# Routed expert block: second group of tiles ranked and scattered before the list begins, copies of the transposes a step later

## The reference, cut to what matters

```python
x = x + tanh(g_xattn) * softmax(mask(scale * (q @ k.T) * layernorm(x)))   # 4 x 512 x 512
h = layernorm(x)                                          # 2048 tokens of 512
w = sigmoid(h @ Wg.T); top 2 of 8 experts by w + bias     # weights divided by their sum
y = sum over a token's two experts: w_e * (silu(h @ W1_e.T) * (h @ W3_e.T)) @ W2_e.T
x = x + tanh(g_ffn) * y
```

## Time and profile before

| | |
|---|---|
| median of 3 timed runs | 350.49 us (348.11 to 350.96) |
| the profiled execution's own time | 346.8 us |
| its span | 344.9 us |
| TensorE matmuls busy | 286.4 us (83%) |
| VectorE, ScalarE, GpSimd busy | 191.1, 127.8, 195.0 us |
| software DMA queue (GpSimd's) | 9760 packets, 20.49 MB, 38.6% of 16 engines |

### The profile page before, as it was taken

The page is one execution under the profiler, slowest core; times in us unless marked ns, Lnnn a source line. Parts: engine busy times, 40 slices in busy tenths (PEclk is TensorE's granted clock), DMA queues, the critical chain, the costliest instruction groups (busy, mean ns, idle before and its releaser), DMA issues.

```text
span 344.9 us, 5188 instructions
## 1 busy us (share of the span) xinstructions
PE 286.4 (83%) x1316; PEld 204.4 (59%) x1316; DVE 191.1 (55%) x496; ACT 127.8 (37%) x239; POOL 195.0 (57%) x208
## 2 busy tenths in 40 slices
PE   4889898489876497678776799999999999999981
PEld 1244454245435375565564577888888888888860
DVE  2697868999946287565233325454454454454530
ACT  2678577237626233022122122333323333323320
POOL 5198997266884616616587355635656535664313
PEclk9999899658865599989989999999999999999998
DMA  7999889955833521945669376856666654865345
GB/s 225 331 416 323 269 291 361 291 184 134 158 105 93 141 74 8 62 57 93 63 66 97 30 121 119 130 115 121 114 104 107 115 105 80 153 112 104 56 62 61
DMA packets 27026, 48.69 MB, mean 141 GB/s; under 512 B 9524, under 2 KB 10296, under 8 KB 25976
## 3 DMA queue, kind: packets, MB, share of 16 engines
q0 software_dynamic: 9760, 20.49, 38.6%
q1 hardware_dynamic: 14408, 15.04, 13.6%
q10 hardware_dynamic: 2832, 12.85, 12.3%
HBM read 28.51 MB, written 19.85 MB: 140 GB/s over the span
## 4 chain that ended last, share of the span: by engine, by line
DMA 47%; issue 22%; POOL 12%; DVE 9%; PE 5%; POOLq 2%; ACT 1%; SPq 1%; ACTq 0%; DVEq 0%
DMA out<-rows,slot 29%; DMA out<-rows 8%; POOL rows L439 5%; DMA slot_table<-entry,slot_index 4%; POOL out L458 3%; DMA rows<-in_x 3%; POOL slot_table L426 3%; PE bank L895 2%; DVE rows L691 1%; DVE w_lo L830 1%; POOLq L450 1%; DMA rows<-xn_rows,slot 1%; DMA w_hi<-in_ctx_t 1%; DVE w_hi L668 1%; DVE bn L661 1%
## 5 line engine op out<-in xcount | busy, mean ns | idle before, releaser
L458 POOL DMA_INDIRECT out<-rows,slot x39 | 62.1, 1592 | 75.0 <-DMA out<-rows,slot 37.4
L809 DVE TENSOR_TENSOR xt_lo<-bank,xt_hi 128x512 fp32r<-128x512 f32 x39 | 27.0, 691 | 77.6 <-ACT xt_hi L581 66.3
L984 PE MATMUL bank<-w_hi,xt_hi 128*128 x156 | 65.2, 418 | 0.6 <-issue 0.6
L986 PE MATMUL bank<-w_hi,xt_lo 128*128 x156 | 61.4, 394 | 0.0
L985 PE MATMUL bank<-w_lo,xt_hi 128*128 x156 | 61.4, 393 | 0.0
L602 ACT ACTIVATE rows<-bank,slot 128x512 f32<-128x512 f32 x39 | 26.8, 688 | 73.9 <-DMA out<-rows,slot 40.1
L439 POOL DMA_INDIRECT rows<-xn_rows,slot x39 | 39.2, 1004 | 22.9 <-issue 15.2
L589 ACT ACTIVATE rows<-bank 128x256 f32<-128x256 f32 x39 | 15.0, 385 | 81.2 <-PE bank L986 60.7
L426 POOL DMA_INDIRECT slot_table<-entry,slot_index x32 | 32.9, 1028 | 17.5 <-issue 8.9
L1011 PE MATMUL bank<-w_hi,gt_hi 128*128 x78 | 31.7, 406 | 13.3 <-DVE gt_lo L826 13.3
L815 DVE SCALAR_TENSOR_TENSOR rows<-rows,bank 128x256 f32<-128x256 f32 x39 | 16.3, 418 | 34.5 <-ACT rows L589 32.1
(11 more groups left out here) (128 smaller groups left out, 464.6 us busy)
## 6 DMA issues: line engine op xcount, KB each, us to landing
w_lo<-in_w ACTq DMA_DIRECT2D x8, 1024.0 KB, 7.0
xn_rows<-w_hi SPq DMA_DIRECT2D x17, 256.0 KB, 8.9
rows<-in_x SPq DMA_DIRECT2D x16, 256.0 KB, 4.7
out<-rows SPq DMA_DIRECT2D x16, 256.0 KB, 4.0
w_lo<-in_w ACTq DMA_DIRECT2D x8, 512.0 KB, 5.8
w_hi<-in_ctx_t SPq DMA_DIRECT2D x4, 256.0 KB, 5.4
slot<-slot_table SPq DMA_DIRECT2D x39, 1.0 KB, 2.7
rows<-xn_rows,slot POOLq DMA_INDIRECT x39
```

Of the source, the lines that this page charges most:

```text
L458: pool.indirect_dma_start(out=out[0:SPARE + P * READY[segment(i)], :], out_offset=bass.IndirectOffsetOnAxis(ap=slot[:, i, 0:1].bitcast(U32 ...
L809: dve.tensor_tensor(xt_lo[:, i % 2].rearrange("p k s -> p (k s)"), ps_x[i % 2][:], xt_hi[:, i % 2].rearrange("p k s -> p (k s)").bitcast(F32),
L984: pe.matmul(ps_h[i % 2][:], xt_hi[:, i % 2, k, :], hi, start=(k == 0), stop=False)
L986: mm = pe.matmul(ps_h[i % 2][:], xt_lo[:, i % 2, k, :], hi, start=False, stop=(k == KC - 1))
```

## The change

- The scatters of group 0 are issued in steps 9 to 12 instead of 10 to 13 (`SCATTERS`). SyncE waits for them and loads the slots of the first seven entries one step sooner, ahead of its store of tile 14.
- Group 1 is ranked, weighted and given its slots by VectorE right behind the last residual, before the low parts of the first two gathered entries and the last splits. TensorE counts its positions behind the first gathered transpose, into a bank of their own. GpSimd issues six of its eight scatters behind gather 3 (new call), the other two with entry 0, ahead of addition 0.
- Group 2's ten scatters are spread over entries 4 to 10 (2, 1, 2, 1, 2, 1, 1) instead of 4 to 8 (two each).
- ScalarE copies the transposes of a tile one step later, right behind the exponentials; TensorE makes the logits of a tile behind the spins instead of at the step's start. One weight piece is split a step sooner, and the splits stand ahead of the router's tanh.

```diff
--- before.py
+++ after.py
@@ -52,13 +52,13 @@
     READY = (7, 11, TILES)
     UNITS = 3 * E
     PIECE = W13 // 2
-    SPLITS = (1, 1, 2, 2, 1, 2, 1, 2, 1, 1, 1, 2, 1, 1, 1, 2)
+    SPLITS = (1, 1, 2, 2, 1, 2, 1, 2, 1, 1, 1, 2, 1, 1, 2, 1)
     LO_BY_POOL = (0, 1, 2, 4, 6, 7, 9, 10)
     LOADS = {0: (2,), 1: (3,), 2: (4,), 4: (5,), 5: (6,), 6: (7,), 7: (8,), 8: (9, 10, 11), 9: (12,), 10: (13,), 11: (14,),
              12: (15,)}
-    SCATTERS = {10: (0, 0, 3), 11: (0, 3, 6), 12: (0, 6, 10), 13: (0, 10, 14)}
-    LATE_SCATTERS = {0: (1, 0, 4), 1: (1, 4, 6), 2: (1, 6, 8), 4: (2, 0, 2), 5: (2, 2, 4), 6: (2, 4, 6), 7: (2, 6, 8),
-                     8: (2, 8, 10)}
+    SCATTERS = {9: (0, 0, 3), 10: (0, 3, 6), 11: (0, 6, 10), 12: (0, 10, 14)}
+    LATE_SCATTERS = {0: (1, 6, 8), 4: (2, 0, 2), 5: (2, 2, 3), 6: (2, 3, 5), 7: (2, 5, 6), 8: (2, 6, 8), 9: (2, 8, 9),
+                     10: (2, 9, 10)}
     SPINS = 5
     SLOT_SEMS = 16
     ROWS = (E - 1) * REGION + LIST * P
@@ -175,7 +175,7 @@
         bank = [psum(f"bank{i}") for i in range(8)]
         ps_s = bank[0:2]
         ps_neg, ps_t, ps_early, ps_q, ps_k, ps_l = bank[2:]
-        ps_pos = (ps_early[:, 0:(MOST + 1) * E],) + 2 * (ps_l[:, 2 * P:2 * P + (MOST + 1) * E],)
+        ps_pos = (ps_early[:, 0:(MOST + 1) * E], ps_neg[:, 0:(MOST + 1) * E], ps_l[:, 2 * P:2 * P + (MOST + 1) * E])
         ps_h = bank[0:2]
         ps_g = bank[2]
         ps_x = (bank[4], bank[6])
@@ -362,7 +362,8 @@
                     store_xn(step - 2)
                 if 2 <= step and step - 2 + XR < TILES:
                     reuse_x(step - 2)
-                if step == TILES:
+                if step == TILES - 1:
+                    listed(0)
                     for i in range(4):
                         load_slots(i)
                 if 1 <= step <= TILES:
@@ -370,8 +371,6 @@
                 if step % NT == 3 and step // NT + 2 < B:
                     load_ctx(step // NT + 2)
                 if step == TILES - 1:
-                    listed(0)
-                elif step == TILES:
                     for i in range(4, FIRST[1]):
                         load_slots(i)
             for k in (1, 2):
@@ -503,6 +502,7 @@
             normed(TILES - 1)
             gather(2)
             gather(3)
+            enter_slots(1, 0, 6)
             for i in range(LIST):
                 if i + 4 < LIST:
                     gather(i + 4)
@@ -625,19 +625,23 @@
             act.activation(tg[:], gb_sb[:, 0:2], ACT.Tanh).then_inc(s_tg, 1)
             for step in range(TILES):
                 exponentials(step)
+                if step >= 2:
+                    transposed(step - 2)
+                for unit in units_in(step)[0:2]:
+                    if unit != 2 * E + 4:
+                        split_hi(unit)
                 if step == END[0] + 1:
                     router_tanh(0)
                 elif step == END[1] + 1:
                     router_tanh(1)
-                for unit in units_in(step):
-                    split_hi(unit)
                 squares(step)
-                if step >= 1:
-                    transposed(step - 1)
+                if step == TILES - 2:
+                    split_hi(2 * E + 4)
                 if step % NT == 2 and step // NT + 1 < B:
                     project(step // NT + 1)
                 for n in LOADS.get(step, ()):
                     load_weights(n)
+            transposed(TILES - 2)
             split_hi(UNITS - 2)
             gathered_hi(0)
             transposed(TILES - 1)
@@ -859,23 +863,19 @@
                 elif step == END[0] + 2:
                     router_slots(0)
                     list_tiles(0)
-            for unit in units_in(TILES - 1):
+            router_ranks(1)
+            router_weights(1)
+            gathered_lo(0)
+            router_slots(1)
+            gathered_lo(1)
+            for unit in range(2 * E + 5, UNITS):
                 split_lo(unit)
-            gathered_lo(0)
-            split_lo(UNITS - 2)
-            gathered_lo(1)
-            split_lo(UNITS - 1)
-            router_ranks(1)
             for i in range(LIST):
                 gate_rows(i)
                 if i + 2 < LIST:
                     gathered_lo(i + 2)
-                if i == 0:
-                    router_weights(1)
                 gated_transposed(i)
                 if i == 0:
-                    router_slots(1)
-                elif i == 1:
                     list_tiles(1)
                 elif i == 2:
                     router_ranks(2)
@@ -941,6 +941,8 @@
                 counts = where[:, n * E:(n + 1) * E]
                 pe.wait_ge(s_chosen, 3 * g + 3)
                 pe.wait_ge(s_slots, 2 * g)
+                if g == 1:
+                    pe.wait_ge(s_zmax, TILES)
                 pe.matmul(counts, ones[:], chosen_sum[:], start=True, stop=False)
                 for t in range(n):
                     pe.matmul(counts, ones[:], chosen[:, start + t, :], start=False, stop=(t == n - 1))
@@ -991,7 +993,7 @@
                 if i > 0:
                     pe.wait_ge(s_gt, 2 * i)
                 else:
-                    pe.wait_ge(s_zmax, TILES)
+                    pe.wait_ge(s_slots, 4)
                 for c in range(FC):
                     mm = pe.transpose(ps_g[:, c * P:(c + 1) * P], gate[:, i % 2, c * P:(c + 1) * P], ident[:])
                 mm.then_inc(s_g, 1)
@@ -1023,8 +1025,6 @@
             pe.wait_ge(s_wg_in, 16)
             projected = 1
             for step in range(TILES):
-                if step >= 2:
-                    logits(step - 2)
                 if step + 1 < TILES:
                     scores(step + 1)
                     masks(step + 1)
@@ -1032,6 +1032,8 @@
                     positions(0)
                 if step < TILES - 2:
                     spin(projected)
+                if step >= 2:
+                    logits(step - 2)
                 if step >= 1:
                     transpose(step - 1)
                 if step % NT == 2 and step // NT + 1 < B:
@@ -1039,6 +1041,7 @@
                     projected += 1
             logits(TILES - 2)
             gathered(0)
+            positions(1)
             transpose(TILES - 1)
             gathered(1)
             pe.wait_ge(s_lo_pool, len(LO_BY_POOL))
@@ -1052,7 +1055,6 @@
                     gathered(2)
                 elif i == 1:
                     gate_transpose(0)
-                    positions(1)
                     gathered(3)
                     output(0, last)
                     gate_transpose(1)
```

## The result

The changed kernel takes 337.88 us (median of 4 runs, 335.28 to 338.05) against 349.30 us for the kernel before (4 runs, 348.11 to 350.96): a ratio of 0.9637, 95% interval 0.9571 to 0.9702, or 11.4 us less. The direction held. The profiled execution of after took 335.28 us with a span of 333.3, 11.6 us less span than before.

What follows compares the result with a forecast made beforehand. Bound: the chain of scatter-additions until entry 11, TensorE behind it. The ruling V falls from 210.6 to 203.55, 7.0 us, taking the profiled 346.8 to 339.8 and the median to 343.5; own range 340 to 347, wide range 336.5 to 351.

Steps and rivals of the forecast that it cites:

- V(11): V for addition 11, landing at 213.35 us: 203.55, forecast to rule in place of addition 8's 210.6.
- V: Earliest place of entry 11 on TensorE's 4.76 us line if addition a lands at t: t + 4.5 - 4.76 (a - 8).
- gather 7's wait: GpSimd's 5.41 us stall for group 1's slots before gather 7, forecast to go.
- new wait at gather 15: GpSimd idles some 6 us for the slots of group 2's last scatter, gather 15 going at 201.45 us.
- cost of additions 3 to 8 behind scatters: List, GpSimd: 7.46 us per addition behind a pair, 6.65 behind one scatter, 42.3 in all; addition 8 lands at 194.1.
- Gather 0 goes at about 107: Start of the list: group 0's last scatter issued near 96, landing 5.6 us later; gather 0 at 107 instead of 113.33.
- The main loop: Later copies, logits and earlier scatters: net taken as 0, bounds 2 us earlier to 3.5 us later.
- ScalarE's wait at L544 near 98 gone: Sign that the forecast is right: ScalarE no longer waits 3.53 us for tile 12's transpose in the main loop.
- Quick: Rival, chance 0.20: a single scatter among additions costs the chain nothing and lands like a gather; 336.5 to 340 us.
- no stall at gather 15: Sign that the forecast is wrong and the quick rival holds: GpSimd does not wait before gather 15.
- Flat: Rival, chance 0.22: main loop costs 3.5 us and the list starts later; 3.5 us won, 347, down to nothing.
- slower: Rival, chance 0.13: scatter ahead of gather 15, single scatters hold every addition 8.86 us; 4.1 us slower, 354.6 us.

Runs made afterwards that it cites:

- u_second: Changed kernel with group 1 ranked and scattered where it was before, all else as changed: 346.65 us, ratio 0.993 to the kernel before.
- only_second: Kernel before with group 1's part of the change alone: 338.26 us against 348.14, ratio 0.973.
- only_spread: Kernel before with group 2's scatters spread as in the change, nothing else: 350.70 us against 347.58, ratio 1.008.
- no_scatter2: Changed kernel without group 2's ten scatters and SyncE's wait for them, leaving out some tokens' expert rows: 324.03 us, ratio 0.930 to the kernel before.
- u_spread: Changed kernel with group 2's scatters in pairs at entries 4 to 8 again: 336.89 us, ratio 0.963 to the kernel before.
- sooner: Changed kernel with group 2's scatter pattern one entry sooner, entries 3 to 9: 337.98 us, ratio 0.970 to the kernel before.
- after_again: The changed kernel run again, unaltered, beside sooner_again on the same chip: 337.01 us, ratio 0.972 to the kernel before.
- sooner_again: The kernel of sooner (group 2's scatters at entries 3 to 9) rerun beside after_again: 335.42 us, ratio 0.966 to the kernel before.
- u_early0: Changed kernel with group 0's scatters back in steps 10 to 13 and SyncE's order as before: 346.52 us, ratio 0.990 to the kernel before.
- second_copy: Changed kernel with group 0's scatters and SyncE's order as before and group 2 in pairs: 342.03 us, ratio 0.976 to the kernel before.
- u_copy: Changed kernel with ScalarE's copies, TensorE's logits and the splits back where they were: 340.54 us, ratio 0.966 to the kernel before.

## Why the prediction was right in kind and short in size

| step | forecast us | measured us |
|---|---|---|
| last residual | 109 | 107.4 |
| gather 0 | 107 | 109.2 |
| first hidden matmul | 117.8 | 117.2 |
| slots(1) done | 116.9 | 116.5 |
| addition 0 issued | 130.5 | 131.2 |
| addition 2 issued | 146.9 | 145.9 |
| addition 8 issued | 188.25 | 185.0 |
| last scatter | 191.45 | 188.2 |
| gather 15 (its wait) | 201.45 (6) | 196.7 (5.6) |
| addition 11 issued | 208.45 | 203.85 |
| V(11), which rules | 203.55 | 199.0 |

**Right.** The chain of additions as the bound, V as the number to carry, group 1's slots and scatters ahead of addition 0, the end of gather 7's wait, the new wait at gather 15, and addition 11 taking the rule from addition 8 all came as written. u_second and only_second show on the chip that group 1's part carries the gain (8.8 us lost without it, 9.9 us won by it alone), and only_spread that the late scatter ahead of gather 15 is a price (3.1 us by the medians, 1.5 of them behind addition 0).

**The term that was mis-sized.** The step of the forecast that failed is the cost of additions 3 to 8 behind scatters, 42.3 us, where 38.8 were measured. "An addition behind a pair of scatters costs (200.2 - 162.9) / 5 = 7.46 us of chain, one without 5.86", and from these 6.65 for one behind a single scatter. In after, additions 4, 6 and 8, with one scatter ahead, land 5.5, 3.9 and 5.4 us behind the one before (mean 4.9, under the lower bound of 5.86), additions 3, 5 and 7, with two, 8.2, 8.1 and 7.7. The six together take 38.8 us to land instead of 42.3, and the single ones are the reason: 14.8 us against 3 x 6.65 = 19.95, while the three behind two scatters took 24.0 against 3 x 7.46 = 22.4. The floor was wrong: 5.86 was a single row, of an addition that is issued only when the one before it has landed (7 at 200.15, 8 at 200.96). Additions 4 and 8 of after do the same and still take 5.5 and 5.4. Others overlap: 6 is issued at 170.10, while 5 lands at 172.55. no_scatter2 shows what six periods cost without scatters, 27.8 / 6 = 4.6 us, and the other kernels 1.25 to 1.51 us for each scatter on top, with about 0.1 between single ones and pairs. With u_spread's 1.39 us, which owes nothing to after, the same sum is 27.8 + 9 x 1.39 = 40.3, with before's own 1.51 it is 41.4; after measured 39.0 by issue, against 41.35 in the forecast.

**Where the 4.6 us of V went.** Addition 2 was 1.0 us ahead of the forecast: addition 0 landed 0.6 us earlier (7.88 us of flight and not 9.2, from an issue 0.7 us late), and addition 1 flew 4.96 us and not 5.6. The six periods, counted by issue, gave 2.3. From the last scatter to gather 15 took 8.5 us instead of 10.0, another 1.5; that is the second term mis-sized, a landing of 4.67 us and not 5.6 and 3.8 from there to the gather, not 4.4. From there to addition 11 took 7.15 instead of 7.0. The sum is 4.6; the remaining 1.1 us between 343.5 and 337.88 is that the median stood 2.6 us above the profiled execution here, not 3.7.

**Right sum, wrong reason.** "Gather 0 goes at about 107" failed: the last scatter of group 0 was indeed issued near 96, at 95.67, but SyncE's slot loads came only at 106.15, 10.5 us behind, not 5.6. In before it was 8.2 us from 102.12. The 5.6 us were not the landing: that piece of the chain ends at 107.72, where GpSimd finishes tile 14's normed row. SyncE itself was held by these scatters from 105.80, for 3.1 us, until 108.9, so in before they took 6.8 us to land. Its wait there (engine, line, releaser: us in total, times, longest):

```profile
SPq L321 <- DMA slot_table<-entry,slot_index: 3.1, 1, 3.1
```

Issued one step sooner they take still longer. By SyncE's waits it is 9.5 us in after, 9.1 in u_second, 9.0 in no_scatter2, 9.9 in sooner, 10.7 in after_again (only sooner_again has less, 8.2 at most) and most in u_spread, whose chain of waits has

```profile
94.68 13.29 DMA slot_table<-entry,slot_index
```

In only_second, u_early0 and second_copy, where the last of them stands in step 13 as in before, it is 5.6 to 6.8 us. The scatters of steps 11 and 12 now go out beside two stores and a weight load, issued at 91.5 to 91.9; that these delay them was not tried. So 6.45 us sooner in issue made 4.1 us sooner in gather 0. It cost little because TensorE was with tile 14's logits until 111.6 in any case, and waited 1.4 us for the gathered rows behind them.

**The main loop**, taken as 0, cannot be read better than that: u_copy and after do not differ by what the runs tell, and one program's loop varies by 7 us (106.4 to 113.5), more than the bounds of 2 us earlier and 3.5 later that were given. "ScalarE's wait at L544 near 98 gone" was wrong in part: the copy of that transpose still waits 2.04 us, but behind the exponential, which no longer waits for it.

```profile
100.45 0.59 ACT L544 COPY w_hi<-bank 128x512 f32<-128x512 f32 x1 [2.04 <-PE bank L924]
```

**The rivals.** Quick had the size (336.5 to 340 for the time) and the better numbers on two terms: 8.2 us from the last scatter to gather 15 (8.5 measured) and 40.0 for additions 3 to 8 (38.8). It did not have the mechanism: a single scatter does cost something, and no stall at gather 15, named as its sign, did not come true (its own sum has one). That its sum came near is luck in part: additions behind two scatters cost more than it took, those behind one less. The forecast's own working took 5.6 us for the last landing; the scatter at 188.19, 7.7 us behind the one before it, took 4.67 us to land, and 4.9 to 5.55 us at the same place in after_again, u_early0, u_second, u_copy and only_spread. The Trainium skill (DMA: Bandwidth & Descriptors, section on the anatomy of one DMA) gives 2.0 us plus bytes over 436 GB/s for a DMA issued by GpSimd, an estimate of 2.0 us for the scatter's 1 KB. The 4.67 us are more than twice that; the measurement decides. Flat and slower did not come; the last scatter was issued at 188.2, well ahead of the 196.0 from which slower would have decided.

What also was not foreseen: the forecast added the parts as if each kept its own worth. They do not add. Group 1's part alone wins 9.9 us and the full change 11.4, yet taking group 0's early scatters out of the full change costs 8.6, and the spread alone loses 3.1. With the later copies the list begins late unless group 0's table is early. And the spread costs 3 to 5 us where group 0's scatters are late (u_early0 against second_copy) and nothing that can be seen where they are early (after against u_spread); why, no run shows.

## What to carry to other kernels

Where a chain of dependent accumulating DMAs sets the pace, look for everything that one engine's queue puts ahead of it and between its links, and for what that waits for. Here the queue stood 8.57 us for group 1's slots with the first addition behind it; ranking group 1 10 to 14 us sooner, so that its eight small scatters go out before the list's additions begin, was worth 9.9 us alone. Take the price of such an instruction from a mean over many periods with it and a mean over many without it, not from one row as floor, and see what paces the periods without it. And when a producer is spread out to be cheaper, follow its last piece to the reader that waits for all of it.

## What the runs showed of the hardware that was not expected

A scatter of 1 KB (128 entries of 8 bytes) slows the list by 1.25 to 1.51 us while additions set its pace, and ten of them take 12 to 14 us of 338, although they move 10 KB in all. The landing time of the same transfer was 4.67 to 5.55 us for the last scatter of group 2 in six kernels, 8.07 us for the one at 144.22 in before, and 9.0 to 13.3 us in six kernels for the last of group 0 where it is issued in step 12, near SyncE's stores (94.68 to 107.99 in u_spread). In after an addition's flight was 4.7 to 5.0 us with nothing near it, 6.3 right behind a single scatter, though with another addition in flight too, and 6.9 to 7.9 behind two or more; the longest, with pairs, were 10.12 us (184.15 in before) and 10.71 (178.03 in second_copy). Making the descriptors is not constant either: the second and third scatter at 118.04 and 120.02 took 1.67 and 1.95 us where the others of the burst take 0.97, and the same two did so in each kernel with six scatters behind gather 3 (1.53 to 1.76 and 1.95 to 1.96). What slows those two is open.
